# A macaron block in fp32 on one core: the feed-forward stages' four batches taken in turn within a cycle, and their side work at new places

## The reference

```python
x = x + 0.5 * ffn(_layernorm(x))
x = x + attn(_layernorm(x))
x = x + 0.5 * ffn(_layernorm(x))
```

```python
gf = _global_net(x.mean(axis=1, keepdims=True), ...)   # 256 -> 128 -> 64 -> 1
out = x
for _ in range(3):                                     # NUM_CYCLES
    tf = _coupling_net(out, ...)                       # 256 -> 256 -> 128 -> 64 -> 1
    combined = 0.7 * gf + 0.3 * tf
    coupling = 0.1 + adaptive_range * (combined - 0.5) * 2.0
    out = out + coupling * _twist(out)
```

## Time and profile before

| | us |
|---|---|
| median of 3 runs | 1358.92 |
| lowest, highest | 1358.5, 1360.76 |
| the profiled execution, its own time | 1361.13 |
| its span | 1359.1 |
| PE busy | 1133.3 (83%) |
| DVE busy | 1149.4 (85%) |
| ACT busy | 737.0 (54%) |
| POOL busy | 871.9 (64%) |
| granted TensorE clock, mean over the span | 0.949 |

### The profile page before, as it was taken

One profiled execution on the slowest core, in us unless ns is written; L12 is line 12 of the kernel. 1 busy time (PEld: TensorE's weight loads), 2 busy tenths in 40 slices (PEclk: granted clock), 3 DMA queues, 4 the chain that ended last, 5 costly groups with the idle time before them and its releaser, 6 DMA issues. The chain is left out here.

```text
span 1359.1 us, 10889 instructions
## 1 busy us (share of the span) xinstructions
PE 1133.3 (83%) x2880; PEld 491.7 (36%) x2880; DVE 1149.4 (85%) x1628; ACT 737.0 (54%) x1267; POOL 871.9 (64%) x390
## 2 busy tenths in 40 slices
PE   3999985769778889878978987987896978799997
PEld 2344432223333334324324333433432423434443
DVE  4656676399999999999999999999999999746556
ACT  2554444757655756755656674665674433355442
POOL 0000000699989999998999999899999998000000
PEclk9999996798999999999999989999998988999998
DMA  6000000444535444354453544435435442000001
GB/s 201 0 1 1 0 0 1 140 135 146 180 102 185 132 149 155 124 185 134 146 179 113 174 146 139 151 124 186 154 127 184 155 156 78 0 0 0 32 31 62
DMA packets 46940, 146.47 MB, mean 108 GB/s; under 512 B 4448, under 2 KB 13280, under 8 KB 46880
## 3 DMA queue, kind: packets, MB, share of 16 engines
q1 hardware_dynamic: 46384, 144.96, 31.8%
q10 hardware_dynamic: 496, 0.82, 0.2%
HBM read 141.05 MB, written 4.72 MB: 107 GB/s over the span
## 5 line engine op out<-in xcount | busy, mean ns | idle before, releaser
L905 POOL TENSOR_TENSOR m_u<-m_dx,m_brow 128x1024 f32<-128x1024 f32 x256 | 596.7, 2355 | 1.0 <-DVE m_a_bank L988 0.9
L791 ACT ACTIVATE m_a_bank<-m_delta,m_negA 128x512 f32<-128x512 f32 x512 | 335.0, 683 | 171.6 <-DVE m_hc L1000 131.3
L1134 PE MATMUL m_y_bank<-m_hc,ident 128*128 128x512 f32 x640 | 333.1, 646 | 103.7 <-DVE m_hc L1000 103.7
L917 POOL TENSOR_TENSOR m_hc_pool<-m_hid,m_crow 128x1024 f32<-128x1024 f32 x96 | 226.0, 2354 | 28.5 <-DVE m_hid L988 28.1
L1134 PEld LDWEIGHTS m_y_bank<-m_hc,ident 128*128 128x128 f32 x640 | 120.1, 201 | 290.7 <-DVE m_hc L1000 170.5
L1000 DVE TENSOR_TENSOR m_hc<-m_a_bank,m_crow 128x512 f32<-128x512 f32 x320 | 202.5, 673 | 0.0
L926 POOL TENSOR_TENSOR m_dx<-m_delta,m_x 128x1024 f32<-128x1024 f32 x16 | 37.7, 2357 | 249.5 <-ACT m_delta L863 249.5
L988 DVE TENSOR_TENSOR_SCAN m_a_bank<-m_a_bank,m_carry,m_u 128x512 f32<-128x512 f32 x160 | 196.1, 1270 | 1.1 <-ACT m_a_bank L791 0.8
L988 DVE TENSOR_TENSOR_SCAN m_a_bank<-m_a_bank,m_u 128x512 f32<-128x512 f32 x160 | 186.6, 1212 | 7.1 <-POOL m_u L905 3.5
L1134 PE MATMUL m_y_bank<-m_hc_pool,ident 128*128 128x512 f32 x384 | 184.4, 603 | 5.6 <-POOL m_hc_pool L917 5.6
L333 PE MATMUL f_bank<-f_state,w 128*128 128x512 f32 x384 | 181.9, 603 | 0.0
(11 more groups left out here) (111 smaller groups left out, 1168.8 us busy)
## 6 DMA issues: line engine op xcount, KB each, us to landing
m_brow<-bc_rows SPq DMA_DIRECT2D x128, 512.0 KB, 4.8
m_crow<-bc_rows SPq DMA_DIRECT2D x128, 512.0 KB, 3.9
x_tok<-x_in SPq DMA_DIRECT2D x4, 1024.0 KB, 8.6
out<-x_tok SPq DMA_DIRECT2D x3, 1024.0 KB, 4.4
w<-w_in SPq DMA_DIRECT2D x1, 1024.0 KB, 11.4
out<-x_tok SPq DMA_DIRECT2D x2, 512.0 KB, 3.0
w<-w_in SPq DMA_DIRECT2D x1, 750.0 KB, 10.4
w<-w_in ACTq DMA_DIRECT2D x1, 512.0 KB, 5.9
```

Of the source, the lines that this page charges most:

```text
L791: nc.scalar.activation(a_bank[K % 2][:, j, :], delta[:, i % 2, c, :], ACT.Exp, scale=negA[:, c, n:n + 1]).then_inc(S["a"], 1)
L905: nc.gpsimd.tensor_tensor(u[:, K % U_RING, :, :], dx[:, i % 2, 2 * q:2 * q + 2, :], brow[:, K // 2 % ROW_RING, K % 2, :].unsqueeze(1).to_b ...
L917: nc.gpsimd.tensor_tensor(hc_pool[:, before % POOL_RING, :, :], hid[:, before % POOL_RING, :, :], crow[:, K // 2 % ROW_RING, K % 2, :].uns ...
L1134: op = nc.tensor.matmul(y_bank[:, j, :], ident[:, :], source[:, before % ring, j, :], start=False, stop=K % PASS == PASS - 1)
```

## The change

The four batches go through a cycle in turn: steps 0 to 3 are the first cycle of batches 0 to 3, steps 4 to 7 the second, 8 to 11 the third. A batch's steps are so four apart, and before two. All "in" work comes in steps 0 to 2, all "g" work in steps 0 to 3, and "back" of batches 0 and 1 in steps 10 and 11 at places 0, 1, 2, 3, of batches 2 and 3 behind step 11. `z_tok` has eight tiles in place of four. DVE's list and the place of one ACT instruction follow; of the statistics, batch 0's are taken in step 11, batch 1's behind it ahead of the last update, batch 2's behind the last update.

```diff
     def batch(s):
-        return s // (2 * CYCLES) * 2 + s % 2
+        return s % BATCH
 
     def cycle(s):
-        return s % (2 * CYCLES) // 2
+        return s // BATCH
+
+    LAST = STEPS - BATCH
...
-    WORK += [(6, 0, "back", 0, 0), (6, 1, "back", 0, 1), (6, 4, "back", 0, 2), (7, 0, "back", 0, 3)]
...
+    for b in range(1, BATCH):
+        WORK += [(b - 1, t, "in", b, t) for t in range(BT // 2)]
+        WORK += [(b - 1, 3, "g", b - 1, 0), (b - 1, 4, "g", b - 1, 1), (b, 0, "g", b - 1, 2)]
+    WORK += [(3, 2, "g", 3, 0), (3, 3, "g", 3, 1), (3, 4, "g", 3, 2)]
+    WORK += [(LAST + 2, t, "back", 0, t) for t in range(BT // 2)]
+    WORK += [(LAST + 3, t, "back", 1, t) for t in range(BT // 2)]
+    WORK += [(TAIL, 0, "back", 2, t) for t in range(BT // 2)]
+    WORK += [(TAIL, 1, "back", 3, t) for t in range(BT // 2)]
+    WORK = sorted(WORK, key=lambda w: w[:2])
...
-        return t if (kind, b) in (("in", 0), ("back", 2), ("back", 3)) and (b, t) != (2, 0) else 7
+        return t if (kind, b) in (("in", 0), ("back", 2), ("back", 3)) else 7
...
-        z_tok = sb("z_tok", [P, 4, DIM])
+        z_tok = sb("z_tok", [P, BT, DIM])
...
             moments_of((2, 3))
+            invert((2, 3))
+            for t in range(4):
+                normalise(2, t)
             sum_up(1)
...
-            for s in range(STEPS + 1):
+            for s in range(1, STEPS + 1):
                 adds(s, (0,) if s == TAIL else (0, 1))
                 if s == TAIL and measure_next:
-                    measure(2)
-                if s > 0:
-                    for h in range(HALVES):
-                        update(s - 1, h)
+                    measure(1)
+                if s <= BATCH:
+                    coupling_base(s - 1)
+                for h in range(HALVES):
+                    update(s - 1, h)
...
                 if s < TAIL:
-                    adds(s, (4,))
+                    adds(s, (2, 3, 4))
+                if s == LAST + 3 and measure_next:
+                    measure(0)
+            if measure_next:
+                measure(2)
             for t in range(4):
                 add_back(3, t)
...
-                    pe.wait_ge(updated, updates(s - 2, h))
+                    pe.wait_ge(updated, updates(s - BATCH, h))
...
                 read(s, 3)
+                if s == 0:
+                    deviation((2, 3), 3)
                 gelu2(s, 0)
```

More of the change, by code:

```diff
@@ L199, in normalise @@
                 o = b * BT + 2 * t
-                if (b, t) >= (0, 2):
-                    earlier = (b, t - 2) if t >= 2 else (b - 1, t + 2)
-                    dve.wait_ge(work_done, done_count(("in",) + earlier))
+                if b > 0:
+                    dve.wait_ge(work_done, done_count(("in", b - 1, t)))
                 for i in range(2):
-                    last = nc.vector.tensor_scalar(z_tok[:, (2 * t + i) % 4, :], x_tok[:, o + i, :],
+                    last = nc.vector.tensor_scalar(z_tok[:, 2 * t + i, :], x_tok[:, o + i, :],
                                                    moments[:, o + i, 0:1], rstd[:, o + i:o + i + 1],
@@ L267, in _ @@
             invert((1,))
-            normalise(1, 0)
-            normalise(1, 1)
+            for t in range(4):
+                normalise(1, t)
             sum_up(0)
-            normalise(1, 2)
-            normalise(1, 3)
             if load_sem is not None:
@@ L280, in _ @@
             moments_of((2, 3))
+            invert((2, 3))
+            for t in range(4):
+                normalise(2, t)
             sum_up(1)
-            coupling_base(0)
             def adds(s, places):
@@ L287, in adds @@
                             add_back(b, t)
-            for s in range(STEPS + 1):
+            for s in range(1, STEPS + 1):
                 adds(s, (0,) if s == TAIL else (0, 1))
                 if s == TAIL and measure_next:
-                    measure(2)
-                if s > 0:
-                    for h in range(HALVES):
-                        update(s - 1, h)
-                if s == 1:
[L297 to L311, removed]
-                if s < TAIL:
-                    adds(s, (4,))
+                    measure(1)
[3 more added lines that the diff above has]
+                    update(s - 1, h)
+                if s == 1:
+                    for t in range(4):
+                        normalise(3, t)
+                if s in (1, 2):
+                    sum_up(s + 1)
+                if s < TAIL:
+                    adds(s, (2, 3, 4))
[3 more added lines that the diff above has]
+                measure(2)
             for t in range(4):
@@ L378, in work @@
                             last = nc.tensor.transpose(out[:, (2 * k + i) * P:(2 * k + i + 1) * P],
-                                                       z_tok[:, (2 * t + i) % 4, k * P:(k + 1) * P], ident[:, :])
+                                                       z_tok[:, 2 * t + i, k * P:(k + 1) * P], ident[:, :])
                 elif kind == "back":
@@ L501, in _ @@
                 read(s, 1)
-                if s == 1:
-                    deviation((2, 3), 3)
                 gelu1(s, 1, 0)
```

## The result

| | before | after |
|---|---|---|
| median of 4 runs, us | 1358.91 | 1388.92 |
| ratio after / before, 95% interval | | 1.0217 (1.0197 to 1.0237) |
| the profiled execution: time, span | 1361.13, 1359.1 | 1388.53, 1386.7 |
| PE busy, DVE busy | 1133.3, 1149.4 | 1139.2, 1149.0 |

A forecast was written before the change was run, and what follows sets the result against it. PE was taken to bound the feed-forward stages; front +4.0, waits +15.6, clock +8.0 and first stage's end +3.4 sum to +31.0 on the 1358.92 us median: 1389.9, so 1390, range 1379 to 1398.

The forecast's parts named there:

- waits with a fallen clock: Main forecast: PE idles at place 3 and its clock then falls; 1385 to 1394 us, chance 0.64.
- front: pairs in bank 7, less the 1.14: Steps 0 to 2: new waits for ACT to free bank 7, less a vanished step 1 wait; +4.0 us, both stages.
- the wait at place 3, four times: Steps 10 and 11, both stages: fourth back unit waits for DVE's add behind the update; 3.9 us each, +15.6.
- the clock behind it: After each place-3 wait PE runs at half clock for a while; 2.0 us each, +8.0, with ends 0 and 12.
- end of the first stage: DVE's closing chain gains one add and one measure, less PE arriving 0.50 earlier; +3.4 us.
- end of the second stage: No measure there, and the fourth add fits into the wait for tanh; 0 us.
- the first pair: Place 3, "in" then "g" in bank 7: 0.83 us wait, two more a stage, +1.66.
- the second: Place 0 of steps 1 and 2, "g" then "in" in bank 7: +0.74 us, twice, +1.5 a stage.
- Rival (B): The place-3 waits don't come; only front and end costs remain, 1366.3 us; chance 0.04.
- Rival (A): The place-3 waits come but PE's clock holds; 1381.9 us; chance 0.15.
- the prediction's own signs of being wrong: Place-3 idle times under 2 us, clock staying full behind them, or PE idling in steps 3 to 9.
- The lower bound: Least clock loss behind a place-3 wait: nothing lost, from the next four instructions after 2.28 us idle.

The follow-up runs named there:

- e6: The kernel before, with only ACT's square root for batches 2 and 3 and its table loads moved into step 0: 1358.52 us, ratio 0.9989.
- e1: The changed kernel, with DVE's add of the place-2 unit ahead of the update in steps 10 and 11 instead of behind it: 1368.40 us.
- e4: The kernel before, old batch order, with batch 0's four back units at places 0 to 3 of step 6 and DVE's adds as in the change: 1372.42 us.
- e2: The changed kernel, with four unread matmuls on PE ahead of the place-3 unit in steps 10 and 11, filling the wait: 1381.47 us.
- e5: The kernel of e1, with the statistics of batches 0, 1 and 2 each taken one place earlier: 1365.23 us.
- e3: The changed kernel, with the fourth back unit of batches 0 and 1 at place 4 instead of 3: 1377.01 us.

## Why the prediction was right

Its forecast was the likeliest case, waits with a fallen clock, at 1390; the chance for slower was 0.98. Step by step, both stages together, the terms as predicted and as the trace of the changed kernel has them. A wait can be counted there in two ways: by its idle time in brackets, or by how much later the next group starts than it would without it. The second is a little more, since an idle time begins only at the modelled end of the last matmul, where the next group would have overlapped it.

| term | predicted | trace, waits by idle time | trace, waits by starts |
|---|---|---|---|
| front: pairs in bank 7, less the 1.14 | +4.0 | +3.6 | +4.4 |
| the wait at place 3, four times | +15.6 | +14.9 | +15.6 |
| the clock behind it | +8.0 | +6.2 | +6.2 |
| end of the first stage | +3.4 | +2.9 | +2.9 |
| end of the second stage | 0 | +0.3 | +0.3 |
| sum (of the terms before rounding) | +31.0 | +27.9 | +29.3 |

**Front.** Two more waits of 0.83 and two of 0.63 a stage came and the 1.14 went: 1.78 a stage by idle time. By starts the first pair costs 0.98 (33.86 to 35.28 in place of 0.44) and the second 0.70. I had the second, counted by starts, at 0.74, and the first at its idle time: that is where the term was 0.4 too low. The root and its loads stayed hidden, as e6 shows.

**The wait at place 3.** Right in place, cause and size. PE's product before it starts at 174.27 and the unit at 179.88, 5.61 later in place of 1.72: 3.89, against 3.9 predicted, of which 3.73 show as idle time. e1 and e4 show the cause from both sides: the add's place in DVE's list makes it or takes it away, with either order of the batches. Rival (B), that it would not come, is out.

**The clock.** Right in kind (e2) and too high in size. I took 2.0 for each; the trace has 2.8, 0, 1.7 and 1.7. The row of 4.18 us idle had 1.7, which two of the four repeat to the tenth. Rival (A), that the clock holds, was right for one wait of four, and a clock that stays full was one of the prediction's own signs of being wrong. The lower bound was read too narrowly: it rests on one wait of 2.28 us without a loss, but the same trace of before has two waits of 1.91 us ahead of the same matmuls, one with a loss and one without:

```profile
324.71 3.78 PE L1122 MATMUL m_y_bank<-m_x,m_diag_d 128*128 128x512 f32 x4 [1.91 <-DVE m_gate L1010]
550.12 1.98 PE L1122 MATMUL m_y_bank<-m_x,m_diag_d 128*128 128x512 f32 x4 [1.91 <-DVE m_gate L1010]
```

Behind the first the granted clock is 0.50 from 324 to 330, and these four and the next four matmuls lose 2.9 us together. So a fall after some waits of 2 us, and a loss above 2.0, could have been read there. The figure of the Trainium skill (TensorE: Matmul & The Clock Gate, HAM oscillation) gave 0.8 for each; all three falls were dearer, and one wait had no fall at all, where the example starts cold every time. In that example each burst of work is short and the next wait follows; here PE has work that goes on for longer. That this makes the difference is likely, but no run here tests it.

**Ends.** From the start of the last layer3 to DVE's last statistics the first stage took 19.44 us before (194.77 to 214.21) and takes 22.76 (205.90 to 228.66), less the 0.44 of the unit that no longer stands ahead: 2.9. The prediction's 3.4 left out that the last four adds, behind the new `measure`, no longer wait for PE's transposes and take 0.44 less. e5 confirms that a `measure` stands on this path, though taking it out gave 2.6 by the traces and not its full 3.3. In the second stage the extra unit delayed tanh by what it saved ahead, and 0.3 is left in the last transfers.

**What the sum missed.** By starts the terms give 29.3, and the two profiled spans differ by 27.6. Three stretches that no term foresaw make the rest, -1.7 together: PE came to the first stage's second "in" unit 1.2 us earlier (27.33 against 28.54), the Mamba block took 1.0 less, and the second stage's first matmuls 0.5 more (5.99 us against 5.52 to the second "in" unit). With them the trace is accounted for to 0.1. The medians differ by 30.0, the profiled executions' times by 27.4: that of before was 2.2 above its median, that of the change 0.4 below.

So the mechanism was right, but that the forecast came within about 1 us is partly luck. The clock was 1.8 and the first end 0.5 too high, the front 0.4 too low, and against the profiled times, from which the terms were read, the sum of 31.0 is 3.6 too high; the medians happened to lie further apart than these.

## What to carry to other kernels

When producer and consumer share one buffer, the wait is set by where the releasing instruction stands in the other engine's list, not by how long it takes: here 0.68 us of work behind 6.2 us of an update. Before moving work to an earlier place, look up in the other engine's order what stands ahead of its release. And count an idle time of PE of 2 to 4 us as more than its length: in these traces five of eight such waits (of 2.02 in e3 and 3.73 in the change) were followed by 1.7 to 2.8 us of loss at the half clock, and the two of 4.4 in e4 by 1.3 and 2.5.

## What the runs showed of the hardware

- Idle times of PE of the same length, 2.02 us in e3, brought a fall of the clock in two of four cases and none in the others; of 3.73 us, in three of four; of 4.4 us (e4), in both. In the kernel before two of 1.91 us ahead of the same matmuls differ in the same way. The length alone does not decide.
- Work whose result nobody reads kept the clock at full (e2) and made the program 7.5 us faster by the medians than the change without it.
- A table load of ACT (1.28 us) ahead of an instruction that waits for data runs before that wait ends (e6: load at 37.61, root at 39.64), so this load costs nothing where the instruction has to wait anyway. The load back (39.97) comes behind the instruction and is not covered by that wait.
